# Local attention normalised ahead of its transposes, and steps cut finer under a new list, in an adaLN block of two attentions

## What is computed

```python
h = layernorm(x) * (1 + ca) + sa
x = x + ga * attention(h)                  # 16 heads of 8, causal, 512 keys
h = layernorm(x) * (1 + cb) + sb
for l in range(2):                         # the second block, DEPTH = 2
    t = shift_token(h)                     # half of the channels one token later
    q, k, v = split(t @ wqkv[l])           # 8 heads of 64
    q, k = rotary(l2norm(q) * qs, l2norm(k) * ks)
    h = h + local_attention(q, k, v) @ wo[l]
    t = layernorm(shift_token(h)) * lg + lb
    a, g = split(t @ w1[l] + b1[l])        # 2 x 341
    h = h + (a * gelu(g)) @ w2[l] + b2[l]
x = x + gb * h
```

## Time and profile before

| | |
|---|---|
| median of 3 runs | 2433.9 us (2421.71, 2433.9, 2438.56) |
| the profiled execution | 2427.62 us, its span 2425.8 us |
| mean granted clock of TensorE | 0.979 |
| busy: PE, DVE, ACT, POOL | 2183.1, 1646.6, 1587.9, 563.6 us |
| HBM read and written | 11.40 and 4.19 MB |

### The profile page before, as it was taken

How to read it: one execution, slowest core, us unless ns; L and a number is a source line. 1 busy time by engine, 2 the same in 40 slices (tenths; PEclk the granted TensorE clock), 3 DMA queues, 4 the chain that set the end, 5 groups by cost and what they waited for, 6 DMA issues and landing times. The chain is left out here.

```text
span 2425.8 us, 52449 instructions
## 1 busy us (share of the span) xinstructions
PE 2183.1 (90%) x21002; PEld 1383.2 (57%) x21002; DVE 1646.6 (68%) x2617; ACT 1587.9 (65%) x3047; POOL 563.6 (23%) x528
## 2 busy tenths in 40 slices
PE   3599899998999899998999989999899989999897
PEld 2455656556565466655565555655656546666454
DVE  2465877676866768667776676776776676866664
ACT  1267766767667676676666776667766767667664
POOL 2012330222302412024210243012330231202410
PEclk9799999999999999999999999999999999999998
DMA  3300132001320012100220012300131001320001
GB/s 100 61 9 17 32 58 43 2 17 37 58 39 17 14 35 54 31 17 16 51 55 12 17 32 46 50 6 17 37 53 43 17 1 37 52 36 18 16 17 25
DMA packets 62521, 78.67 MB, mean 32 GB/s; under 512 B 9266, under 2 KB 57004, under 8 KB 59948
## 3 DMA queue, kind: packets, MB, share of 16 engines
q1 hardware_dynamic: 62284, 75.33, 16.0%
HBM read 11.40 MB, written 4.19 MB: 6 GB/s over the span
## 5 line engine op out<-in xcount | busy, mean ns | idle before, releaser
L872 DVE TENSOR_REDUCE nm<-ps 128x2 f32<-128x768 f32 (+3 forms) x384 | 388.4, 1042 | 121.6 <-PE ps L562 114.8
L1009 POOL TENSOR_TENSOR pr<-pr 128x1024 f32<-128x1024 f32 x128 | 302.2, 2361 | 678.9 <-DVE pr L910 678.9
L805 ACT ACTIVATE pr<-ps,wb,inv 128x128 f32<-128x128 f32 x1024 | 370.6, 490 | 97.8 <-DVE wb L927 97.8
L505 PE MATMUL ps<-cf,pr 128*128 128x128 f32 x2048 | 284.6, 279 | 100.4 <-POOL pr L1019 69.0
L505 PEld LDWEIGHTS ps<-cf,pr 128*128 128x128 f32 x2048 | 225.7, 141 | 161.9 <-POOL pr L1019 81.7
L762 ACT ACTIVATE pr<-ps 128x896 f32<-128x896 f32 x256 | 233.4, 921 | 70.3 <-PE ps L580 67.0
L903 DVE TENSOR_TENSOR pr<-ps,rot 128x1024 f32<-128x1024 f32 x128 | 156.5, 1223 | 149.2 <-ACT pr L777 143.7
L777 ACT ACTIVATE pr<-ps 128x1024 f32<-128x1024 f32 x128 | 131.1, 1025 | 143.8 <-PE ps L628 81.4
L580 PE MATMUL ps<-Q,K 128*128 128x512 bf16 (+3 forms) x1024 | 223.7, 299 | 0.0
L561 PE MATMUL ps<-K,Q 128*128 128x128 bf16 x1024 | 196.6, 222 | 28.2 <-DMA K<-Kf 25.3
L921 DVE TENSOR_REDUCE wm<-ps 128x8 f32<-128x1024 f32 x128 | 156.7, 1224 | 69.0 <-PE ps L659 68.0
(11 more groups left out here) (151 smaller groups left out, 4453.3 us busy)
## 6 DMA issues: line engine op xcount, KB each, us to landing
pr<-V SPq DMA_DIRECT2D x32, 520.0 KB, 4.7
Q<-Kf SPq DMA_DIRECT2D x224, 64.0 KB
K<-Kf SPq DMA_DIRECT2D x224, 64.0 KB
pr<-V SPq DMA_DIRECT2D x32, 390.0 KB, 6.2
xn<-in_L_attn_x SPq DMA_DIRECT2D x16, 256.0 KB, 2.8
out<-hT SPq DMA_DIRECT2D x16, 256.0 KB, 2.2
Q<-in_c_edge SPq DMA_DIRECT2D x32, 64.0 KB
Q<-mT SPq DMA_DIRECT2D x128, 4.0 KB
```

The lines of the kernel that those rows point to most:

```text
L505: mm = pe.transpose(dst[:, t * P:(t + 1) * P], src(t), ident)
L805: ins = act.activation(P2[s][:, 2 * (p % 2) + r, o:o + P], bank[:, r * T + o:r * T + o + P], ACT.Exp, scale=inv[s][:, t, h:h + 1], bias=wb ...
L872: dve.tensor_reduce(nm[s][:, qt, h0:h0 + n], src, AX_X, ALU.max, negate=True).then_inc(nm_r[s], 1)
L1009: pool.tensor_tensor(t1[s][t % 3], t1[s][t % 3], t2[s], ALU.add).then_inc(sum_r[s], 1)
```

## The change

Three things change together.

1. Steps are cut finer. `qkv` becomes `qkv`, `rotate` (DVE, POOL) and `v`; `heads` becomes `qheads` and `kheads`; `spread` hands its DVE part to `scale`; `score` hands the last two key tiles of two heads to `tail`; `proj` goes one half at a time; the exponents leave `wscore` for `wexp(l, p, r)`, one head at a time, and so does `pturn(l, p, r)`. A step's work is the same, it only stands elsewhere.
2. A new table `PLACES` permutes the list of one sample, and `ALL` and `FIRST_BANKS` are new to go with it.
3. The local attention is normalised earlier. The exponents' instruction also gives the sum of its row (`accum_out`); a step `share` takes the reciprocals on DVE and multiplies the exponents by them on POOL, before `pturn`. In `wctx` V is now the stationary operand and the turned exponents move, so the context comes out by channels, both heads in one bank, and ACT copies it straight to `ctx2`. `wturn`, `tok`, the column of ones of V and its memset are gone. `P2` has room for three p.

```diff
-            out += [("wscore", l, p)] * (p < NP2) + [("wctx", l, p - 2)] * (2 <= p <= NP2 + 1)
-            out += [("pturn", l, p - 1)] * (1 <= p <= NP2) + [("wturn", l, p - 3)] * (p >= 3)
-        out += [("wout", l), ("center", 2 + l), ("spread", 2 + l)]
+            out += [("wscore", l, p), ("wexp", l, p, 0), ("share", l, p, 0), ("wexp", l, p, 1), ("share", l, p, 1)] * (p < NP2)
+            out += [("wctx", l, p - 2)] * (p >= 2) + [("pturn", l, p - 1, r) for r in range(2)] * (1 <= p <= NP2)
+        out += [("wout", l), ("center", 2 + l), ("spread", 2 + l), ("scale", 2 + l)]
...
+PLACES = [
+    0, 2, 1, 4, 5, 9, 10, 3, 15, 6, 7, 8, 11, 16, 17, 18, 12, 19, 20, 13, 14, 21, 23, 24, 22, 25, 26, 27, 28, 30,
...
-    rest = [iter([[(s + S2 * (k - back), name) for back, name in names[i:j]] for k in range(B // S2 + 1)
-                  for i, j in zip(firsts, firsts[1:])]) for s in range(S2)]
+    groups = [names[i:j] for i, j in zip(firsts, firsts[1:])]
+    rest = [iter([[(s + S2 * (k - back), name) for back, name in groups[i]] for k in range(B // S2 + 1) for i in PLACES])
+            for s in range(S2)]
...
-        P2 = [a[:, 0:4 * T].rearrange("p (i n) -> p i n", n=T) for a in flat]
+        P2 = [[a[:, i * T:(i + 1) * T] for i in range(4)] + [c[:, :], d[:, 4 * T:5 * T]] for a, c, d in zip(flat, y, scr)]
...
 PE
-                        for r in range(2):
-                            bank, full = banks.take(pe, (b, "pturn", l, p, r), [pt_r.at(b, 2 * n + r + 1)])
-                            pe.wait_ge(*we_r.at(b, 2 * n + r + 1))
-                            transposes(bank, lambda t: P2[s][:, 2 * (p % 2) + r, t * P:(t + 1) * P]).then_inc(full, 1)
+                        bank, full = banks.take(pe, (b, "pturn", l, p, r), [pt_r.at(b, 2 * n + r + 1)])
+                        pe.wait_ge(*part_r.at(b, 2 * n + r + 1))
+                        transposes(bank, lambda t: P2[s][2 * (p % 3) + r][:, t * P:(t + 1) * P]).then_inc(full, 1)
...
-                            for j in range(NT):
-                                for half, val in enumerate((VB, V2)):
-                                    q0 = j * P + half * D2
-                                    mm = pe.matmul(bank[D2 * half:D2 * half + D2, j * (D2 + 1):(j + 1) * (D2 + 1)],
-                                                   PT[s][:, (2 * n + r) % 3, q0:q0 + D2], val[s][:, j, 2 * p + r, :],
-                                                   start=True, stop=True, skip_group_check=True)
-                            mm.then_inc(full, 1)
-                    elif kind == "wturn":
-                        l, p = a
-                        n = NP2 * l + p
-                        bank, full = banks.take(pe, (b, "wturn", l, p), [c2_r.at(b, n + 1)])
-                        pe.wait_ge(*tok_r.at(b, 2 * n + 2))
-                        transposes(bank, lambda t: tok[s][n % 2][:, t, :]).then_inc(full, 1)
+                        for t in range(NT):
+                            for half, val in enumerate((VB, V2)):
+                                q0 = t * P + half * D2
+                                for r in range(2):
+                                    mm = pe.matmul(bank[D2 * r:D2 * r + D2, q0:q0 + D2], val[s][:, t, 2 * p + r, :],
+                                                   PT[s][:, (2 * n + r) % 3, q0:q0 + D2], start=True, stop=True,
+                                                   skip_group_check=True)
+                        mm.then_inc(full, 1)
...
 ACT
+                        if p >= 3:
+                            banks.wait(act, (b, "pturn", l, p - 3, r))
+                        for t in range(NT):
+                            o, h = t * P, 2 * p + r
+                            ins = act.activation(P2[s][2 * (p % 3) + r][:, o:o + P], bank[:, r * T + o:r * T + o + P], ACT.Exp,
+                                                 scale=inv[s][:, t, h:h + 1], bias=wb2[s][:, t, h:h + 1],
+                                                 accum_out=sums[s][:, t, h:h + 1])
+                        ins.then_inc(we_r[s], 1)
...
 DVE
-                            dve.reciprocal(rec2[s][:, r, :], bank[:, :, D2]).then_inc(rd_r[s], 1)
-                            dve.wait_ge(*rd_r.at(b, 2 * n + r + 1))
-                            dve.tensor_tensor(tok[s][n % 2][:, :, r * D2:(r + 1) * D2], bank[:, :, 0:D2],
-                                              rec2[s][:, r, :].unsqueeze(2).broadcast_to([P, NT, D2]),
-                                              ALU.mult).then_inc(tok_r[s], 1)
+                    elif kind == "share":
+                        l, p, r = a
+                        n, h = 2 * (NP2 * l + p) + r, 2 * p + r
+                        dve.wait_ge(*we_r.at(b, n + 1))
+                        if n >= H2 or b >= S2:
+                            dve.wait_ge(*part_r.at(b, n - H2 + 1))
+                        dve.reciprocal(shares[s][:, :, h], sums[s][:, :, h]).then_inc(share_r[s], 1)
...
 POOL
+                        pool.wait_ge(*share_r.at(b, n + 1))
+                        part = P2[s][2 * (p % 3) + r].rearrange("p (t n) -> p t n", t=NT)
+                        share = shares[s][:, :, h].unsqueeze(2).broadcast_to([P, NT, P])
+                        pool.tensor_tensor(part, part, share, ALU.mult).then_inc(part_r[s], 1)
```

More of the change, by code:

```diff
@@ L54 @@
 SPREADS = 16 * 2 * (2 * SLOTS + 1)
-SHIFTS = {("spread", 1): 0, ("wout", 0): 1, ("down", 0): 2, ("wout", 1): 3}
+SHIFTS = {("scale", 1): 0, ("wout", 0): 1, ("down", 0): 2, ("wout", 1): 3}
 def steps():
@@ L67, in steps @@
         for j in range(4):
-            out += later[j + j // 2:j + 1 + (j + 1) // 2] + [("score", 4 * g + j)]
+            out += later[j + j // 2:j + 1 + (j + 1) // 2] + [("score", 4 * g + j)] + [("tail", 2 * g + j // 2)] * (j % 2)
             if j == 0 and g:
@@ L80, in steps @@
         out += [("hid", l, c) for c in range(3)] + [("down", l)]
     out += [("final",)]
[L82 to L87, removed]
@@ L88, in steps @@
-    return between + [(0, name) for name in out[:cut]]
[L94 to L99, removed]
+    cut = out.index(("pturn", DEPTH - 1, NP2 - 1, 1)) + 1
@@ new lines, in steps @@
+    first = {("pturn", DEPTH - 1, NP2 - 1, 1): [("load",)], ("wctx", DEPTH - 1, NP2 - 1): [("center", 0)],
+             ("wout", DEPTH - 1): [("spread", 0), ("scale", 0)], ("scale", 1 + DEPTH): [("proj", 0), ("proj", 1)]}
+    between = [(0, name) for name in first[out[cut - 1]]]
+    for last in out[cut:]:
+        between += [(1, last)] + [(0, name) for name in first.get(last, [])]
+    return between + [(0, name) for name in out[:cut]]
+PLACES = [
[8 rows of a table added]
+]
+ALL = ("153200001057408000684f9856edbbaffea95b4440e9d01082041156797bd765051965bfbf53d4802082884ed7d7e6366e67fffbef68"
+       "59889000970978c56edbbaffe995ac48169d01044042155b9dd6f55049c27bfebd726804082484e6f5fe47672e7fffbef391588a0009"
+       "b0978c56edbbaffec973504169d0110204115679dbcfa184956abfbb9dac804082484ecebfec3a5d67fffbef3a1588a0009b0978c56e"
+       "dbbaffe98f3490169d01104042155b9bdd75305252e7f7eadca804082884eaf5fe6367367fffbef6919889000970978c56edbbaffe98"
+       "db190159d0110404215579bdaf54844d373fbda7b8804082884eaef7e4b66ce7fffbef691988c000750978c56edbbaffea95b910169d"
+       "01104042155b9ee9f3504c55abf7eb9a6204042884eaedfe9363d4ffffbef391588c0009b0978c56edbbaffea95ad10169d011020421"
+       "55d97dd75485164dbf7daed4404043084ecf77e33a3d5bfffbef688b489000970978a56edbbaffe98db450159d01082042155b9bbdd3"
+       "184c666bfdd9db48040830a4ab73fec5663ceafbf4fbe43b2f80124c5095c35d29fd4d6bfbeb3c0e4c7100088244e585eeba11a8977a"
+       "c6aff92bc21017bffffffffffff")
@@ L742, in step @@
                     elif kind == "proj":
-                        for i in range(2):
-                            act.activation(parts[s][3 * i], banks.wait(act, (b, "qk", i)), ACT.Copy).then_inc(hi_r[s], 1)
+                        i, = a
+                        act.activation(parts[s][3 * i], banks.wait(act, (b, "qk", i)), ACT.Copy).then_inc(hi_r[s], 1)
                     elif kind == "values":
```

271 lines of the change are left out of this document (133 added, 138 removed), and 7 rows, old and new, of the table PLACES.

## The result

The changed kernel takes 2369.99 us (median of four runs, 2360.03 to 2381.49), the kernel before beside it 2431.68: a ratio of 0.975, 95% interval 0.972 to 0.978, 62 us less. The forecast was 2407. The time lies in the range given, and the gain is more than twice the 27 us that I had worked out. The profiled execution is the slowest of the four, 2381.49 us, and the profiled one of before took 2427.62, so the account by the two traces has 46 us to explain.

The account below looks back on a forecast made before the run. TensorE, busy 90%, was taken to bound the kernel, with three engines near their limit in the exponent stretches. 2427.6 - 70 + 89 + 4 - 50 = 2400.6, plus 6 for the runs' median: 2407 us; range 2335 to 2490.

Parts of the forecast that it names:

- TensorE's work, -70: 128 second turns of the context go and its product narrows from 65 to 64 columns: 70 us less, 77 with drains.
- The price of a row sum, 0.09 us: Each of 1024 local-attention exponents on ScalarE takes 0.09 us more for its row sum, 11.5 us per pair of samples.
- Rival (a): The row sum on ScalarE is nearly free, giving 2333 us; chance 0.20.
- rival (b): The row sum costs ScalarE 0.16 us or more in the three stretches, giving 2479 to 2538 us; chance 0.20.
- ScalarE's stretches, +89: ScalarE ends the three stretches of local-attention exponents per pair of samples; TensorE's added waits there cost 89 us.
- 19.9, 39.5 and 19.3 us: Predicted lengths after the change of the three exponent stretches per pair of samples, with the steps ahead and behind.
- a loss of 3.2 us per pair: TensorE's predicted loss in the three exponent stretches before the change, set against 14.3 us per pair after.
- The shared port, +4: VectorE operations with two SBUF inputs and GpSimd's new multiplications exclude each other: 7 us, some waited for, so +4.
- The order, -50 of 120: Finer steps and new order win back 50 us of TensorE's 120 us of waits, mostly outside the exponent stretches.
- Rival (c): The order only moves waits and gives none back, since VectorE's pace in the rotations stays: 2457 us; chance 0.20.
- Waits at the turns of 10 us per pair: Sign: TensorE's waits at `pturn` grow to some 10 us per pair, ended by GpSimd's multiplication.
- signs of being wrong at the root: ScalarE below 90% in the exponent stretches, or TensorE waiting longest elsewhere, for a context copy, exponent buffer or GpSimd's queue.

Follow-up runs that it names:

- The crossings: New arithmetic in the old order (2740.8 us; one place later 2685.9) and old arithmetic in the new order (2509.0; other banks 2448.2).
- slowest crossing: The changed kernel's arithmetic in the order of the kernel before, with its bank choices kept: 2740.8 us, ratio 1.128.

## Why the prediction was right in its main mechanism and wrong in size

- **TensorE's work, -70.** Measured -63: 512 matmuls fewer (21002 to 20490), as counted. Seven more traces have the same matmuls in the same order, and TensorE is busy 2104.2 to 2145.6 us in them, 38 to 79 less than before. That is too wide to tell 70 from 77. Whether TensorE drains at a change of the tiling mode, as TensorEngine Tiling of the Trainium skill, Tiling Modes, says, no run here shows.
- **The price of a row sum, 0.09 us.** Measured 0.092 from start to start, 0.088 from the busy times. Rival (a), nearly free, and rival (b), 0.16 or more, both fall.
- **ScalarE's stretches, +89.** This is the step that failed: it was +42. The lengths came out right. Of the 19.9, 39.5 and 19.3 us of the prediction, 4.4 lie ahead of the first exponent and behind the last (1.21, 1.39, 1.22 and 0.6), so that 15.5, 35.1 and 14.9 are left, and 15.2, 34.7 and 14.8 were measured. Wrong was the work of TensorE set against them. For before I had a loss of 3.2 us per pair, with 32.7 us of work in the 33.0 of the double stretch. But the earlier trace rows show TensorE busy 27.50 us of 30.30 there, and idle 6.5 us in the three windows together; over the whole trace it is 6.3 per pair. For after I had 14.3, which charged the tail behind the last exponent as if nothing else could be done in it; it is 11.6. So about half of the error is the loss of before taken too small, the other half that of after taken too large: 11.6 - 6.3 is +42 for the run. The runs without sums (47 us) and with sums in the kernel before (58 us) confirm the size, and the one without division (4.5 us) shows that the tail is covered.
- **The shared port, +4.** The mechanism of this term did not act. VectorE's L872, formerly L848, does take longer, 1.10 us on the mean of its 48 on tile y, for 0.95 before. But in the run without the multiplications on GpSimd the mean is the same 1.10 us, and in the trace of the changed kernel none of the 64 L872 overlaps a multiplication. The shifts of one row take the same time with and without them (28.8 us in all). As before, 16 of them lie beside the long addition of a rotation (L1025, formerly L1009); the rise goes with the new order.
- **The order, -50 of 120.** Outside the stretches 25 us of idle time went. As a term of a sum it was half as large as I had it; as a term it was also wrongly put. I took the order for a place where waits are recovered, with "none of it back" as the worst end. The crossings show 2686 and 2741 us with the old order: the new chain from exponent to turn doesn't fit there, and worst was some 300 us, not 0. Rival (c) fell, and the end of it that mattered was never among my cases.
- **Luck.** The stretches were 47 us too dear, the order 25 us too generous and TensorE's work 7 us too generous. That the time came within the range owes something to errors that partly cancel.
- **What would show it.** ScalarE over 95% busy in the stretches: yes, 99 to 100%. Transposes 512 fewer, TensorE's idle time grown: yes. Waits at the turns of 10 us per pair, for GpSimd's multiplication: no, 1.6; the idle time inside is spread over many short waits. One of my signs of being wrong at the root did appear: TensorE's longest waits are elsewhere, 25.2 us ahead of the row maxima and 22.0 for the scaling of K in GpSimd's queue. Both are nearly all outside the stretches, so they bear on the order term and not on the price of the sums.

-63 + 42 - 25 is the 46 us between the two profiled executions. The rest of the 62 is that the one after took 11.5 us more than the median of its runs, and the one before 4 us less.

## What to carry to other kernels

When two schedules are compared by hand, open and close the windows at the same event in both, or the tail of one is charged twice. Check TensorE's work in a window against its busy time there before you call the rest a loss. Don't price a new order and new arithmetic apart when they were chosen together: check the arithmetic once in the old order, and the order once with only its bank table exchanged, since here another table for the same order cost 2%. When a term rests on two engines getting in each other's way, look whether the two instructions ever meet. A cost on an engine that ends a stretch shows at more than half its size even where it is only 0.09 us long; it can be moved in part to an engine that has room, but not wholly, if that engine stands in the chain.

## What was new about the hardware

- A row sum with an activation is an instruction of its own in the trace (ACTIVATION_READ_ACCUMULATOR), 244 to 272 ns long in its record, yet it adds 0.092 us to the distance between exponents of 128 columns (0.343 to 0.435 us), since its record overlaps its exponent and the next.
- TensorE's granted clock halved behind waits of no more than 1.59 us each, where they came close together. In the slowest crossing TensorE was busy 150 us more than in the changed kernel on the same matmuls, on top of the waits.
